# Edge scores of two attention layers: the end-of-group signal of TensorE moved from the last product to a drain

## The chip, the cores and the metric

The program runs on one core of one Trainium2 chip. The metric is the device time of one execution in microseconds, lower is better; a kernel's time is the median over its runs. Engines are named as in the profile: PE (TensorE), DVE (VectorE), ACT (ScalarE), POOL (GpSimd) and SP (SyncE).

## The reference

A graph network of four blocks over 3125 nodes with 64 features and 100,000 edges sorted by destination; each block is followed by a residual sum and a layer norm. The change lies in the last block, two GATv2 layers with five heads:

```
xl = (x @ Wl + bl).reshape(n_nodes, H, C)
xr = (x @ Wr + br).reshape(n_nodes, H, C)
e = jax.nn.leaky_relu(xl[src] + xr[dst], NEG_SLOPE)
alpha = jnp.einsum('ehc,hc->eh', e, att)
m = jax.ops.segment_max(alpha, dst, num_segments=n_nodes)
a = jnp.exp(alpha - m[dst])
...
out = jax.ops.segment_sum(a[:, :, None] * xl[src], dst, num_segments=n_nodes)
```

Every node also has an edge to itself. What is computed in the changed stage is `alpha`, the score of each edge and head (and of each self edge).

## The kernel before

The program is one long sequence of phases; each phase is a set of instruction streams, one per engine, that are ordered only by semaphores, and ends with a drain of every engine and a barrier (line 141). The changed function is `gat_edges`, called once by `gat_layer` for each of the two layers.

Edges are laid out in columns of 128 edges (one per partition). There are 816 columns, 32 of them made of nodes whose edges cross a window. A **turn** of the loop takes 24 columns; there are 34 turns a layer. Within a turn:

- **POOL** (line 2503) gathers the source rows of a column from `node_rows` in HBM into `rows_p`, with one indirect DMA per column. `rows_p` has three slots of eight columns. Before a slot is refilled POOL waits until DVE has consumed it (`used`, sent at line 2656), until SP has stored its node features to `x_src` (`stored`), and until the indices are in.
- **ACT** (lines 2594 and 2600) makes `hot_t`, a one-hot matrix of destinations within a window of 128 nodes, for half a turn (12 columns) at a time, with two buffers. Before it writes a buffer it waits until PE is done with that buffer's last group of the turn before, that is, on `made`.
- **PE** (line 2557) multiplies the one-hot matrix with the window's destination rows. These rows are split into three bf16 parts in `parts_r`, so each column takes three products of 330 output columns, accumulated in PSUM. Four columns are a **group** of 12 products; a turn has six groups, numbered 0 to 5. Groups alternate between two halves of `psZ`, so PE may start group n+1 once DVE's product of group n-1 is done (`prod`). The window of a column is known only at run time: at groups 0 and 3 PE's sequencer loads twelve numbers into registers (`pick`, line 2439), and each product's address is formed by a register operation (line 2557). In the first five turns there are two groups more, for the self edges (line 2545: three and two columns, with f32 products); they use no gathered rows.
- **DVE** adds the gathered rows to `psZ` (`add`, line 2646), reduces the group before (`reduce`, line 2669), then multiplies `psZ` after a max with the attention vector into `lz` (`product`, line 2638). The add of a group waits for `made`; the add of the first group of a slot waits for the slot's gathers too; the add of the second waits for nothing but `made` and the engine's own order.

The first five turns and the other 29 are loops of their own on the engines other than PE, which has the five written out. Where in DVE's stream a turn starts can be seen in the trace: there a reduction is followed directly by an add, with no product between them.

PE signals a group by an increment on its last product:

```
last = pe.matmul(psZ[:, n % 2, j, 0:ZH], hot[:, k, col * CE:(col + 1) * CE],
...
last.then_inc(made, 1)
```

and DVE waits with

```
v.wait_ge(made, unit(i, n, early) + EACH)
if at == 0:
    v.wait_ge(got[slot], i * (16 * KS) + 16 * KS)
```

Of the kernel before, what the change touches and what calls it, by code (L numbers as in the profile page):

```python
# [12 lines left out]
NB = N // 125  # L13
NR = P * NB
# [9 lines left out]
CE = 128  # L24
# [25 lines left out]
ZH = H * ZC  # L50
# [2349 lines left out]
def gat_edges(nc, g, h, selfs):  # L2400
# [7 lines left out]
    SB = 5  # L2408
# [8 lines left out]
    with phase(nc) as s:  # L2417
# [3 lines left out]
        locs, hot = s.sb("locs", [WR, 2, KC * CE], u8), s.sb("hot_t", [WR, 2, KC * CE], bf16)  # L2421
        lz = s.sb("lz", [P, 2, G, ZH])
        tab, hT = s.sb("tab_rows", [P, TB, ZH]), s.sb("hT", [P, NR])

        psZ = s.ps("psZ", [P, 2, G, 512])
# [5 lines left out]
        hot_made, made, added, prod, scored, neared = (s.sem(n) for n in ("hot_made", "made", "added", "prod", "scored", "neared"))  # L2431
# [6 lines left out]
        flat = lambda t: t.rearrange("k h c -> k (h c)")  # L2438
# [10 lines left out]
        with nc.Block() as block:  # L2449
# [56 lines left out]
            @block.tensor  # L2506
            def _(pe):

                def copied(by, n):
                    for e in range(2):  # L2510
                        if share(n, e):
                            pe.wait_ge(by[e], share(n, e))

                pe.sem_inc(made, EACH)
                for t, bs in enumerate(batches):
                    if t >= 4:
                        copied(hT_by, t - 3)
                    for b in bs:
                        last = pe.transpose(psZ[0:D, 1, t % 4, (b - bs.start) * P:(b - bs.start + 1) * P], h[:, b, :], g.ident[:, :])
                    last.then_inc(n_turned, 1)  # L2520
                copied(hT_by, len(batches))
                pe.wait_ge(padded, 2)
                for w in range(NWR):
                    if w >= 4:
                        copied(tab_by, w - 3)
                    pe.matmul(psZ[:, 0, w % 4, 0:ZH], hT[:, w * WR:(w + 1) * WR], flat(g.wA[:, :, :]),
                              start=True, stop=True).then_inc(n_source, 1)
                for w in range(NWR):
                    if w >= 4:
                        pe.wait_ge(n_split, w - 3)  # L2530
                    pe.matmul(psZ[:, 1, w % 4, 0:ZH], hT[:, w * WR:(w + 1) * WR], flat(g.wB[:, :, :]),
                              start=True, stop=True).then_inc(n_dest, 1)
                copied(tab_by, NWR)
                pe.wait_ge(n_split, NWR)
                pe.sem_inc(prod, 2)

                def turn(i, early):
                    for n, (kind, m) in enumerate(EARLY if early else LATE):
                        if kind:
                            lo, hi = SELF[m]  # L2540
                            if m == 0:
                                pe.wait_ge(joined, 1)
                            pe.wait_ge(prod, unit(i, n, early))
                            for b in range(lo, hi):
                                last = pe.matmul(psZ[:, n % 2, b - lo, 0:ZH], hT[:, i * SB + b:NR:NB], flat(g.wB[:, :, :]),
                                                 start=True, stop=True)
                            last.then_inc(made, 1)
                            continue
                        k, c = divmod(m, HALF)
                        if c == 0:  # L2550
                            at = pick((i * 2 + k) * KC)
                            pe.wait_ge(hot_made, i * 2 + k + 3)
                        pe.wait_ge(prod, unit(i, n, early))
                        for j in range(G):
                            col = c * G + j
                            for q in range(3):
                                last = pe.matmul(psZ[:, n % 2, j, 0:ZH], hot[:, k, col * CE:(col + 1) * CE],  # L2557
                                                 parts[:, bass.ds(at[col], 1), q, :].rearrange("p o c -> p (o c)"),
                                                 start=q == 0, stop=q == 2)
                        last.then_inc(made, 1)  # L2560

                for i in range(ST):
                    turn(i, True)
                with pe.Fori(ST, NK // 2) as i:
                    turn(i, False)
# [671 lines left out]
```

## Time and profile before

| | us |
|---|---|
| median of 3 runs | 7766.42 |
| lowest and highest run | 7758.99, 7787.47 |
| span of the profiled execution | 7865.6 |

The profiled execution is one more execution, recorded by the hardware profiler; of it the span is given, and no other time. Busy times of engines are sums over the span: PE 4297.8 us (55%), DVE 4772.7 (61%), ACT 2362.7 (30%), POOL 3733.3 (47%).
```text
span 7865.6 us, 104440 instructions
## 1 busy us (share of the span) xinstructions
PE 4297.8 (55%) x26852; PEld 3458.2 (44%) x26923; DVE 4772.7 (61%) x7334; ACT 2362.7 (30%) x3661; POOL 3733.3 (47%) x4217
## 2 busy tenths in 40 slices
PE   5777777310279545555535444444695444444397
PEld 2677776310179545555523222222683222222396
DVE  4666666688521156566547666666665766666675
ACT  5444444117322145555522111111222111111121
POOL 3666566100200166666625555553654555655363
PEclk9555555555589777777767666666896766666696
DMA  8677777895578533233225656564654666656462
GB/s 313 191 219 212 222 203 226 228 236 191 215 250 307 183 112 115 96 117 114 91 72 147 159 152 156 154 157 119 135 134 114 157 158 155 160 150 158 100 140 75
DMA packets 1472089, 1296.30 MB, mean 165 GB/s; under 512 B 1257993, under 2 KB 1297567, under 8 KB 1459038
## 3 DMA queue, kind: packets, MB, share of 16 engines
q1 hardware_dynamic: 902378, 671.59, 28.5%
q0 software_dynamic: 167008, 441.69, 21.0%
q10 hardware_dynamic: 402580, 181.62, 8.4%
q8 instruction: 48, 0.79, 0.0%
q14 instruction: 75, 0.61, 0.0%
HBM read 942.23 MB, written 351.27 MB: 164 GB/s over the span
## 5 line engine op out<-in xcount | busy, mean ns | idle before, releaser
L2503 POOL DMA_INDIRECT rows_p<-node_rows,stage_i x1632 | 1546.5, 948 | 1228.0 <-issue 978.9
L2557 PE MATMUL psZ<-parts_r,hot_t 128*128 x4896 | 1164.3, 402 | 1360.5 <-DVE lz L2638 867.7
L2557 PEld LDWEIGHTS psZ<-parts_r,hot_t 128*128 128x128 bf16 x4896 | 590.0, 121 | 1938.6 <-issue 1624.4
L2646 DVE TENSOR_TENSOR psZ<-psZ,rows_p 128x1320 f32<-128x1320 f32 x408 | 626.5, 1536 | 768.9 <-remote 283.0
L731 POOL DMA_INDIRECT rows_s<-hpx,hpST x784 | 741.4, 946 | 486.4 <-issue 203.8
L1961 POOL DMA_INDIRECT both<-table,srcI x784 | 741.9, 946 | 431.5 <-issue 211.1
L749 PE MATMUL psP<-window,pair_hot 128*128 x3136 | 701.9, 416 | 249.0 <-ACT pair_hot L771 146.6
L749 PEld LDWEIGHTS psP<-window,pair_hot 128*128 128x128 f32 x3136 | 672.8, 325 | 279.2 <-issue 279.0
L828 DVE SCALAR_TENSOR_TENSOR pair_run<-pair_run,same_c,psP 128x64 f32<-128x64 f32 x1568 | 440.2, 281 | 469.1 <-PE psP L749 209.1
L2953 PE MATMUL ps_steps<-A,xs 128*65 128x125 f32 x5184 | 578.8, 272 | 137.8 <-DVE A L2971 93.1
L2638 DVE SCALAR_TENSOR_TENSOR lz<-psZ,att 128x1320 f32<-128x1320 f32 (+2 forms) x428 | 642.6, 1501 | 8.4
L2953 PEld LDWEIGHTS ps_steps<-A,xs 128*65 128x65 f32 x5184 | 562.9, 138 | 153.5 <-issue 151.5
L2600 ACT ACTIVATE hot_t<-near 128x1536 bf16<-128x1536 bf16 x136 | 201.9, 1485 | 1418.1 <-DMA first_tab<-homeX_i 417.4
L2669 DVE TENSOR_REDUCE sj<-lz 128x1320 f32 x408 | 621.1, 1522 | 11.0
L1997 PE MATMUL psZ<-w,bothT 128*128 128x128 f32 x1568 | 374.3, 328 | 214.0 <-ACT bothT L2030 158.2
L2971 DVE TENSOR_TENSOR A<-hotw,aw 128x3000 f32<-128x3000 f32 x108 | 354.6, 3283 | 195.4 <-PE ps_steps L2953 183.9
L2927 POOL TENSOR_TENSOR acc<-acc,part_w 65x125 f32 x648 | 316.5, 488 | 248.1 <-ACT part_w L2886 155.3
L1724 PE MATMUL psY<-parts,tile 128*125 128x192 bf16 x4200 | 388.5, 251 | 72.9 <-DVE parts L1764 45.2
L2594 ACT ACTIVATE near<-locs,node_lane 128x1536 bf16<-128x1536 uint8 x136 | 214.5, 1577 | 705.6 <-DMA locs<-loc_rows 429.7
L1724 PEld LDWEIGHTS psY<-parts,tile 128*125 128x125 bf16 x4200 | 364.3, 140 | 75.4 <-issue 42.9
L1999 PE MATMUL psZ<-w,eaT 128*128 128x128 f32 x1568 | 370.9, 325 | 8.6 <-issue 8.6
L630 ACT ACTIVATE tile<-psA 128x500 bf16<-128x500 f32 (+1 forms) x294 | 161.6, 562 | 644.5 <-remote 421.8
(545 smaller groups left out, 7260.0 us busy)
## 6 DMA issues: line engine op xcount, KB each, us to landing
tile<-adj SPq DMA_DIRECT2D x168, 781.2 KB, 4.9
xs<-x_src SPq DMA_DIRECT2D x432, 128.0 KB
x_src<-rows_p SPq DMA_DIRECT2D x204, 256.0 KB
hpx<-stage ACTq DMA_DIRECT2D x25, 2048.0 KB
window<-hpx SPq DMA_DIRECT2D x196, 256.0 KB
dst_runs<-pair_run SPq DMA_DIRECT2D x28, 1792.0 KB
eaT<-in_ea SPq DMA_DIRECT2D x28, 1792.0 KB
adj<-tile SPq DMA_DIRECT2D x42, 781.2 KB
```

Source lines behind the costliest of these rows:

```text
L731: pool.indirect_dma_start(rows[:, k, j, :], None, g.hpx, bass.IndirectOffsetOnAxis(g.hpST[:, x * K + j:x * K + j + 1], 0)).then_inc(got[k] ...
L749: last = pe.matmul(pair_sum(n, j), hot[:, n % 2, j * CE:(j + 1) * CE], window[:, n % 2, bass.ds(rel[j], 1), :].rearrange("p o c -> p (o c) ...
L828: v.scalar_tensor_tensor(run[:, k, at, :], run[:, k, at - 1, :] if at else run[:, 1 - k, PC - 1, :], same[:, k, at:at + 1], pair_sum(n, j) ...
L1724: last = pe.matmul(psY[0:TC, k % B, 0:3 * D], tile[:, k, b, :], parts[:, b].rearrange("p n c -> p (n c)"), start=b == 0, stop=b == NB - 1)
L1961: pool.indirect_dma_start(both[:, x % 2, j, D:2 * D], None, g.table, bass.IndirectOffsetOnAxis(g.srcI[:, x * K + j:x * K + j + 1], 0)).the ...
L1997: pe.matmul(psZ[:, q % 4, j, :], bothT[:, q % 2, j, :], w1[:, :], start=False, stop=False, skip_group_check=True)
L2503: pool.indirect_dma_start(rows[:, k, j, :], None, g.node_rows, bass.IndirectOffsetOnAxis(stage[:, k, j:j + 1], 0)).then_inc(got[k], 16)
L2557: last = pe.matmul(psZ[:, n % 2, j, 0:ZH], hot[:, k, col * CE:(col + 1) * CE], parts[:, bass.ds(at[col], 1), q, :].rearrange("p o c -> p ( ...
L2638: return v.scalar_tensor_tensor(out, src, 0.0, att.unsqueeze(1).to_broadcast([P, n, ZH]), ALU.max, ALU.mult)
L2646: v.tensor_tensor(here, here, rows[:, slot, at * G:(at + 1) * G, 0:ZH], ALU.add).then_inc(added, 1)
L2669: v.tensor_reduce(out, lz[:, n % 2, 0:size, :].rearrange("p g (h c) -> p g h c", c=ZC), X, ALU.add).then_inc(scored, 1)
L2953: last = pe.matmul(slot(k, j), xs[:, k, j, e, 0:D + 1], A[:, k, j * EG + e, :], start=e == 0, stop=e == EG - 1)
```

## The change

The increment of `made` is taken off the last product of each group, edge groups and self groups alike, and put on a drain instruction behind it. A drain is executed by PE's sequencer and completes when PE has finished what was issued before it. Nothing else is changed; line numbers stay as they were.

```diff
--- before.py
+++ after.py
@@ -2542,9 +2542,9 @@
                                 pe.wait_ge(joined, 1)
                             pe.wait_ge(prod, unit(i, n, early))
                             for b in range(lo, hi):
-                                last = pe.matmul(psZ[:, n % 2, b - lo, 0:ZH], hT[:, i * SB + b:NR:NB], flat(g.wB[:, :, :]),
+                                pe.matmul(psZ[:, n % 2, b - lo, 0:ZH], hT[:, i * SB + b:NR:NB], flat(g.wB[:, :, :]),
                                                  start=True, stop=True)
-                            last.then_inc(made, 1)
+                            pe.drain().then_inc(made, 1)
                             continue
                         k, c = divmod(m, HALF)
                         if c == 0:
@@ -2554,10 +2554,10 @@
                         for j in range(G):
                             col = c * G + j
                             for q in range(3):
-                                last = pe.matmul(psZ[:, n % 2, j, 0:ZH], hot[:, k, col * CE:(col + 1) * CE],
+                                pe.matmul(psZ[:, n % 2, j, 0:ZH], hot[:, k, col * CE:(col + 1) * CE],
                                                  parts[:, bass.ds(at[col], 1), q, :].rearrange("p o c -> p (o c)"),
                                                  start=q == 0, stop=q == 2)
-                        last.then_inc(made, 1)
+                        pe.drain().then_inc(made, 1)
 
                 for i in range(ST):
                     turn(i, True)
```

## Rows read from the trace of the kernel before

**Rows 1.** The page: span, and two groups of part 5 (columns named below)

Columns: line, engine, operation, out<-in, count; busy us, mean ns of one; idle us before, releaser.

```profile
span 7865.6 us, 104440 instructions
...
L2503 POOL DMA_INDIRECT rows_p<-node_rows,stage_i x1632 | 1546.5, 948 | 1228.0 <-issue 978.9
L2557 PE MATMUL psZ<-parts_r,hot_t 128*128 x4896 | 1164.3, 402 | 1360.5 <-DVE lz L2638 867.7
```

**Rows 2.** L2503 in each layer: duration min/median/max in ns, first and last start

```profile
L2503 POOL DMA_INDIRECT rows_p<-node_rows,stage_i x816: 942/948/958, 4106.3 to 5424.6; - x164
...
L2503 POOL DMA_INDIRECT rows_p<-node_rows,stage_i x816: 942/948/978, 5980.9 to 7301.8; - x164
```

**Rows 3.** L2646 over the span, and what ended the idle time before it (us, times)

```profile
L2646 DVE TENSOR_TENSOR psZ<-psZ,rows_p x408: 1529/1534/1542, 4152.5 to 7323.1; 128x1320 f32<-128x1320 f32 x136
...
  remote: 283.0, 58
  DMA first_tab<-homeX_i: 281.9, 52
  issue: 133.0, 22
  PE psZ L2557: 71.0, 17
```

**Rows 4.** Timeline of all engines, 4600 to 4660 us: start, us, engine, line, idle before

```profile
4608.52 1.53 DVE L2646 TENSOR_TENSOR psZ<-psZ,rows_p 128x1320 f32<-128x1320 f32 x1
...
4610.17 1.53 DVE L2638 SCALAR_TENSOR_TENSOR lz<-psZ,att 128x1320 f32<-128x1320 f32 x1
...
4611.62 1.53 DVE L2646 TENSOR_TENSOR psZ<-psZ,rows_p 128x1320 f32<-128x1320 f32 x1
...
4611.85 2.57 PE L2557 MATMUL psZ<-parts_r,hot_t 128*128 x12 [2.92 <-issue]
...
4614.50 1.52 DVE L2638 SCALAR_TENSOR_TENSOR lz<-psZ,att 128x1320 f32<-128x1320 f32 x1
4614.92 0.95 POOL L2503 DMA_INDIRECT rows_p<-node_rows,stage_i  x1 [0.30 <-issue]
...
4616.16 3.48 PE L2557 MATMUL psZ<-parts_r,hot_t 128*128 x12 [1.75 <-issue]
4616.17 0.95 POOL L2503 DMA_INDIRECT rows_p<-node_rows,stage_i  x1 [0.30 <-issue]
...
4619.29 1.48 ACT L2600 ACTIVATE hot_t<-near 128x1536 bf16<-128x1536 bf16 x1 [11.29 <-remote]
4619.30 1.54 DVE L2646 TENSOR_TENSOR psZ<-psZ,rows_p 128x1320 f32<-128x1320 f32 x1 [3.27 <-remote]
...
4627.99 1.54 DVE L2646 TENSOR_TENSOR psZ<-psZ,rows_p 128x1320 f32<-128x1320 f32 x1 [4.29 <-remote]
...
4630.37 0.95 POOL L2503 DMA_INDIRECT rows_p<-node_rows,stage_i  x1 [5.73 <-issue]
...
4641.17 1.86 PE L2557 MATMUL psZ<-parts_r,hot_t 128*128 x12 [2.45 <-DVE lz L2638]
...
4654.95 1.54 DVE L2646 TENSOR_TENSOR psZ<-psZ,rows_p 128x1320 f32<-128x1320 f32 x1 [9.16 <-remote]
...
4657.37 0.94 POOL L2503 DMA_INDIRECT rows_p<-node_rows,stage_i  x1 [5.53 <-DVEq L2656]
```

**Rows 5.** L2656, DVE's release of a slot: who waited for it (us, times)

```profile
  POOL rows_p L2503: 249.1, 38
```

**Rows 6.** PE's sequencer by line, whole span; the last row from 4616 to 4628 us

```profile
L141 PEldq DRAIN  x47: 8/8/131, 23.4 to 7865.1; - x47
...
L2439 PEldq TENSOR_LOAD <-firsts x136: 3/848/1368, 4146.8 to 7307.2; - x136
...
L2564 PEldq COMPARE_BRANCH  x58: 16/208/838, 4359.5 to 7320.5; - x58
...
L2557 PEldq FUSED_REGOPS  x4896: 2/46/1422, 4149.1 to 7320.3; - x196
...
L2557 PEldq FUSED_REGOPS  x21: 3/46/724, 4616.1 to 4627.9; - x21
```

**Rows 7.** Busy time, granted clock (PEclk) and DMA share in the two gather stretches

```profile
4106.00:5425.00 1319.00, 610.55 (x2491) 313.81 (x2490) 906.86 (x660) 224.92 (x179) 772.66 (x816) 0.68 0.60 155
5981.00:7302.00 1321.00, 617.17 (x2488) 308.94 (x2488) 904.88 (x658) 224.25 (x177) 772.46 (x816) 0.68 0.60 154
```

## What the change should do

> **What bounds the kernel now.** I read the page first. The kernel is no chain of one engine: over the span of 7865.6 us no engine is busy for more than 61%, and the changed line L2557 (PE, 1164.3 us busy in 4896 products) has 1360.5 us of idle time before its products [rows 1]. So PE is not short of time there, and only the moment at which its signal `made` arrives can matter. The costliest group of the page is the gather of L2503 on POOL, in the same loop.
>
> Next I read that gather by layer. Each layer issues 816 gathers, from 4106.3 to 5424.6 us and from 5980.9 to 7301.8 us, so 1318.3 and 1320.9 us [rows 2]. In the timeline two gathers that wait for nothing start 1.25 us apart (4614.92 and 4616.17) [rows 4]. 816 x 1.25 is 1020 us, so the layers spend 298 and 301 us in which POOL had no leave to issue, 599 us in both. DVE's own work is less: one group of four columns costs it an add, a reduction and a product, 4.33 us from one product to the next (4610.17 to 4614.50), so 26.0 us a turn of six groups against 30.1 us for POOL's 24 gathers [rows 4].
>
> What takes POOL's leave away? L2646, the add that reads what PE made, has 768.9 us of idle time before it in 149 stalls: 283.0 + 281.9 + 133.0 + 71.0 us, and the profile names mostly releasers that are not in the loop (remote, a DMA of another stage) [rows 3]. The timeline tells more [rows 4]. The turn starts with the add at 4608.52; 4611.62 is the add of its group 1, 4619.30 of group 2, 4627.99 of group 3. Group 2 was multiplied from 4611.85 for 2.57 us, so its products end at 4614.42 by the profile; its add starts at 4619.30. ACT's hot_t, which waits for `made` of that same group and for no gather, starts at 4619.29, 0.01 us away. Group 3 is the second group of its slot, so its add waits for `made` alone: its products end at 4616.16 + 3.48 = 4619.64, its add starts at 4627.99, 8.35 us later. After it POOL starts the next refill at 4630.37, having been idle for 5.73 us. The same again with the group of 4641.17: end 4643.03, add 4654.95, POOL 4657.37. So **PE's signal arrives 5 to 12 us after the products end** in these places, and through DVE's release of the slot (POOL waited for it by name for 249.1 us [rows 5]) it holds back the gathers. The layer is bound by POOL plus these late signals.
>
> **The change part by part.** Removed: the increment on the last product of 428 groups (2 layers of 204 edge groups and 10 self groups). Added: 428 drains on PE, each with the increment. No order changes, on no engine; no product, load or transfer is added.
>
> *The drain itself.* PE's drains at the ends of phases take 8 ns in the median and 131 ns at most [rows 6]. 428 x 0.008 is 3 us, 428 x 0.131 is 56 us, as bounds; I take 10 us of issue, nearly all in PE's idle time.
>
> *What queues behind it.* Now PE's sequencer issues register operations and loads while the last products still run. After a drain it can't: the wait for `prod`, and at groups 0 and 3 the table load of `pick` (848 ns median, 136 of them) and at the back edge the branch (208 ns, 58 of them), start only when PE is empty [rows 6]. Cover: PE gets leave for the next group every 4.33 us, and a group takes 1.86 us at the full clock and 3.48 us at the low one [rows 4]; the mean grant is 0.68 in these stretches, so 0.36 of the time at 2.4 GHz and 0.64 at 1.2 GHz [rows 7]. Low clock with a table load: 0.14 (from product to PE's start) + 3.48 + 0.1 (drain) + 0.85 + about 0.2 of register work is 4.8 us, 0.4 to 0.5 us over the cover. Without a load: 3.7 us, covered. So at most 136 x 0.45 x 0.64 = 39 us, and 58 x 0.3 x 0.64 = 11 us for back edges, 50 us if all lay on the path; at the low end none does, since DVE has 4.1 us a turn to spare against POOL. I take 10 us.
>
> *When the signal arrives.* This is the open term. Before, PE's array sent it; now its sequencer does, after the array is empty. No drain occurs inside a gather loop of this trace, so I bound it: if the new signal is never late, all 599 us of POOL's lost leave could go; if it is as late as before, 0; if lateness also delays the next group, it costs (below). What speaks for one common cause is that PE's sequencer is itself slowed in the same stretch: from 4616 to 4628 us one of its register operations took 724 ns against a median of 46 [rows 6]. A drain with a signal would pass by the same sequencer. I take 0 for this term as the likeliest.
>
> The Trainium skill (PSUM — Partial Sum Buffer, Engine vs sequencer instructions) says that an increment on the matmul fires at its completion, and that a drain waits until the engine is fully idle; by that rule the drained signal can never come before the old one, and the forecast would be no gain in any case. The trace does not contradict the second half, but shows the old signal 8.35 us behind the profile's end of the products [rows 4]. The skill (Perfetto Trace Analysis, Tensor Engine Instruction) also calls that end an estimate, so the products themselves might be late; then the drain waits for them as well.
>
> Sum: 10 + 10 + 0 = +20 us. The sum is made on the profiled execution; its span is 99 us (1.3%) above the median of 7766.42 us, and I carry the difference over unscaled: **7786 us**. That the median is so near also says that most of the lost time is no product of profiling: without it two layers alone would be 599 us shorter.
>
> **The rivals.** About 0.5% (39 us) is what a measurement can tell from no change.
>
> *A. Same lateness, hidden drain (the forecast).* 7769 to 7872 us by the bounds above (3 + 0 to 56 + 50). Chance 0.42, of it 0.36 within 0.5% and 0.06 slower.
>
> *B. The sequencer's signal is not held up.* Then DVE's stalls go and POOL issues nearly without a break. For it: only PE's signals are late here; DVE's product ending at 4616.02 released PE at 4616.16 in the same stretch [rows 4]. Against it: the slowed register operations. The most is 599 us (7167 us); the store of x_src and the waits for slots remain, so I take 0.7 of it, 419 us: about 7350 us, and from 7200 to 7700 us. Chance 0.33.
>
> *C. Lateness in series (the other side).* Before, PE multiplied group 3 from 4616.16 while the signal of group 2 was still out until 4619.3. If the drain must wait for whatever is held up, group 3 starts only at 4619.3, 3.1 us later, and its own late signal counts from there. It decides where two stalls follow each other, as groups 2 and 3 do; in the printed stretch that is one case in a turn, and with 68 turns, some without, I take 45: 45 x 3.1 is 140 us. If it struck two times a turn it were 420 us. So 7786 + 140 = 7926 us, range 7830 to 8200. Chance 0.20.
>
> *D. The edit does nothing,* since the signal was late for a reason of the receiver (DVE and ACT read the semaphore late) and the drain is hidden: 7766 us. Against it, both started within 0.01 us of each other. Chance 0.05.
>
> **How the numbers follow.** Faster is B, 0.33. Within 0.5% is 0.36 of A and 0.05 of D, 0.41 in all. Slower is 0.06 of A and 0.20 of C, 0.26. The likeliest case gives 7786 us; its own range is 7760 to 7850, the measurement's own spread below and most of the bounds above. Cases of both signs hold half of the chance, so the range must reach into B and C: from 7300 us (a third of B is below, 0.11) to 7950 us (somewhat under half of C is above, 0.08).
>
> **What would show it.** In the changed profile: 428 drains of PE at L2547 and L2560 (if no such rows, D's first half). A: the idle time before L2646 stays near 769 us and the two gather stretches near 1320 us; table loads of L2439 start after the last product's end instead of beside it. B: the idle time before L2646 falls under 200 us and the gather stretches to 1050 to 1150 us; then the forecast was wrong on what holds the signal. C: PE's groups start with the late adds, not 3 us ahead of them, the stalls before L2646 grow to 900 us or more, and the gather stretches are longer than 1380 us. The stages outside the two stretches should not move at all; if they did, the comparison would be one of something else.

## The result and the profile after

The change makes the kernel slower by about one and a half per cent.

| | before | after |
|---|---|---|
| median, us | 7770.84 | 7897.47 |
| runs | 4, 7758.99 to 7787.47 | 4, 7876.42 to 7906.69 |
| ratio after / before | | 1.0149, 95% interval 1.0129 to 1.0169 |
| span of the profiled execution, us | 7865.6 | 7896.1 |

The medians are 127 us apart, the two spans only 30. (The quotient of the two medians is 1.0163; it lies inside the interval of the ratio.) The profiled execution of before is none of its four runs and lies 95 us above their median, that of after within 2 us of its own. So the two profiles understate the difference, and they are read for how things go, less for how much. The ratios further down leave out four executions of 7285 to 12792 us, which took far longer than the others of the same kernel.

The page of the changed kernel, span and groups of part 5 (columns as in [rows 1]):

```profile
span 7896.1 us, 104938 instructions
...
L2503 POOL DMA_INDIRECT rows_p<-node_rows,stage_i x1632 | 1542.2, 945 | 1294.7 <-issue 1049.2
L2557 PE MATMUL psZ<-parts_r,hot_t 128*128 x4896 | 1089.6, 391 | 1482.0 <-issue 1069.9
...
L2646 DVE TENSOR_TENSOR psZ<-psZ,rows_p 128x1320 f32<-128x1320 f32 x408 | 626.4, 1535 | 819.1 <-PEq L2560 689.8
```

No instruction of the two groups became longer: a product takes 391 ns in the mean (before 402), a gather 945 (before 948) [rows 1]. What grew is idle time: before the add of L2646 from 768.9 us [rows 3] to 819.1. Its releasers are now named, and all but 22 stalls end by the drain (us, times):

```profile
  PEq L2560: 689.8, 144
  issue: 128.9, 22
```

The gathers of the two layers, first and last start, against [rows 2]:

```profile
L2503 POOL DMA_INDIRECT rows_p<-node_rows,stage_i x816: 940/946/955, 4085.5 to 5431.7; - x164
...
L2503 POOL DMA_INDIRECT rows_p<-node_rows,stage_i x816: 940/946/971, 5981.6 to 7334.0; - x164
```

1346.2 and 1352.4 us instead of 1318.3 and 1320.9, 59 us more in both. The stages outside did not grow: together they are 29 us shorter, which fits a profiled execution of before that was long everywhere, and not an effect of the change. The drain itself is the surprising row (min/median/max in ns; below it, who waited for it):

```profile
L2560 PEldq DRAIN  x408: 219/2052/14652, 4128.5 to 7352.2; - x136
...
  ACT hot_t L2600: 1529.6, 130
  DVE psZ L2646: 689.8, 144
```

A drain that takes 8 ns in the median at the ends of phases [rows 6] takes 2052 ns in the median here and up to 14652. One of them alone, in the stretch from 4610 to 4620 us:

```profile
L2560 PEldq DRAIN  x1: 9148/9148/9148, 4613.0 to 4613.0; - x1
```

and what stands around it in the timeline (columns as in [rows 4]):

```profile
4607.02 1.53 DVE L2646 TENSOR_TENSOR psZ<-psZ,rows_p 128x1320 f32<-128x1320 f32 x1
...
4611.34 1.53 DVE L2646 TENSOR_TENSOR psZ<-psZ,rows_p 128x1320 f32<-128x1320 f32 x1
...
4611.56 1.86 PE L2557 MATMUL psZ<-parts_r,hot_t 128*128 x12 [2.13 <-DVE lz L2638]
...
4614.21 1.52 DVE L2638 SCALAR_TENSOR_TENSOR lz<-psZ,att 128x1320 f32<-128x1320 f32 x1
...
4622.16 1.54 DVE L2646 TENSOR_TENSOR psZ<-psZ,rows_p 128x1320 f32<-128x1320 f32 x1 [6.43 <-issue]
...
4622.47 3.48 PE L2557 MATMUL psZ<-parts_r,hot_t 128*128 x12 [9.05 <-issue]
...
4627.91 1.48 ACT L2600 ACTIVATE hot_t<-near 128x1536 bf16<-128x1536 bf16 x1 [18.63 <-PEq L2560]
4627.91 1.54 DVE L2646 TENSOR_TENSOR psZ<-psZ,rows_p 128x1320 f32<-128x1320 f32 x1 [1.34 <-PEq L2560]
...
4629.67 3.48 PE L2557 MATMUL psZ<-parts_r,hot_t 128*128 x12 [3.72 <-ACT hot_t L2600]
4630.29 0.94 POOL L2503 DMA_INDIRECT rows_p<-node_rows,stage_i  x1 [5.15 <-issue]
...
4637.65 1.86 PE L2557 MATMUL psZ<-parts_r,hot_t 128*128 x12 [2.05 <-issue]
...
4652.92 1.54 DVE L2646 TENSOR_TENSOR psZ<-psZ,rows_p 128x1320 f32<-128x1320 f32 x1 [11.12 <-PEq L2560]
...
4654.30 3.48 PE L2557 MATMUL psZ<-parts_r,hot_t 128*128 x12 [14.79 <-issue]
...
4657.83 1.54 DVE L2646 TENSOR_TENSOR psZ<-psZ,rows_p 128x1320 f32<-128x1320 f32 x1 [0.51 <-PEq L2560]
```

The adds of 4607.02 and 4611.34 are those of groups 2 and 3; the products from 4611.56 are group 4. By the profile they end at 4613.42. The drain behind them starts at 4613.0, takes 9148 ns, and so ends at 4622.15; DVE's add starts at 4622.16, 8.74 us after the products' modelled end, as late as the signals of the kernel before [rows 4]. So it is not the way of the signal that is slow: PE's own sequencer does not see PE as finished until then.

The second thing to see is the next line of PE. Group 5 had leave from 4615.73 on (the product of 4614.21 + 1.52), but starts at 4622.47. In the kernel before it would have started at once, as the group of 4616.16 did [rows 4]. Its signal then comes at 4627.91, 1.96 us after its end at 4625.95, and DVE has stood still once more. And at 4629.67 PE starts group 0 of the next turn, 1.76 us after the drain: in between lie the branch (208 ns from 4628.1) and the table load (848 ns from 4628.5), with register work around them. The profile names ACT's `hot_t` as the releaser there, but group 0 reads the other buffer, which was ready since 4607.67. At 4652.92 a signal arrives 13.4 us after the products of 4637.65 ended; the next group starts 1.38 us later, ends at 4657.78, and its add waits for it (0.51 us).

### The profile page after: what moved, and what is told of

Same layout as the page of the kernel before. It is cut to its first block and busy times, and to the rows that moved or that the text cites. A ratio compares the mean times of both kernels' runs of the same rounds, so it can differ in the third digit from the quotient of the medians.

```text
span 7896.1 us, 104938 instructions
## 1 busy us (share of the span) xinstructions
PE 4257.9 (54%) x26922; PEld 3469.0 (44%) x26923; DVE 4772.0 (60%) x7334; ACT 2359.9 (30%) x3661; POOL 3724.4 (47%) x4217
## 5 line engine op out<-in xcount | busy, mean ns | idle before, releaser
L2503 POOL DMA_INDIRECT rows_p<-node_rows,stage_i x1632 | 1542.2, 945 | 1294.7 <-issue 1049.2
L2557 PE MATMUL psZ<-parts_r,hot_t 128*128 x4896 | 1089.6, 391 | 1482.0 <-issue 1069.9
L2557 PEld LDWEIGHTS psZ<-parts_r,hot_t 128*128 128x128 bf16 x4896 | 583.8, 119 | 1993.2 <-issue 1675.2
L2646 DVE TENSOR_TENSOR psZ<-psZ,rows_p 128x1320 f32<-128x1320 f32 x408 | 626.4, 1535 | 819.1 <-PEq L2560 689.8
L731 POOL DMA_INDIRECT rows_s<-hpx,hpST x784 | 739.5, 943 | 476.2 <-issue 205.9
```

The lines of the kernel that those rows point to most:

```text
L731: pool.indirect_dma_start(rows[:, k, j, :], None, g.hpx, bass.IndirectOffsetOnAxis(g.hpST[:, x * K + j:x * K + j + 1], 0)).then_inc(got[k] ...
L2503: pool.indirect_dma_start(rows[:, k, j, :], None, g.node_rows, bass.IndirectOffsetOnAxis(stage[:, k, j:j + 1], 0)).then_inc(got[k], 16)
L2646: v.tensor_tensor(here, here, rows[:, slot, at * G:(at + 1) * G, 0:ZH], ALU.add).then_inc(added, 1)
```

## The experiments

Three theories were put to the test. **S (series):** a drain holds PE until its own late completion, so the next group no longer runs under the wait. **L (late signal):** the drain's signal reaches the others later than a product's would. **T (table loads):** the sequencer's work behind a drain is exposed. All are short edits of `gat_edges`.

The runs fell on different chips, and that turned out to matter more than the change: the same kernel before took 7771, 7885 and 7775 us in three sets of runs and 6823 and 6816 us in two others. Every ratio below is against the kernel before on the same chip in the same set. I call the first kind of chip "late" and the second "prompt", after what PE's completions do on them. No chip is known to have served in two sets, so the words name what a set showed and not a proven property of the chip.

**e1: a drain behind each group that signals nothing.**

```diff
                         last.then_inc(made, 1)
+                        pe.drain()
```

(the same behind the self groups)

> The kernel before with a drain behind every group that signals nothing; the last product signals as before. Theory S (series): the cost comes from PE being held at the drain until its own late completion, so the next group is multiplied only after it; then this costs the same as the change, 7870 to 7910 us, and PE's groups start late as in the changed kernel. Theory L (late signal): the drain's own signal reaches DVE and ACT later than a product's would; then the time is that of before, 7760 to 7790 us.

Measured on a prompt chip: 6824.70 us against 6823.01, ratio 1.0010 (1.0001 to 1.0020). It can't tell S from L there. But its profile, of an execution as fast as the kernel before, shows what is different on such a chip. The add's idle time (us, times) in its profile:

```profile
L2648 DVE TENSOR_TENSOR psZ<-psZ,rows_p x408: 1525/1530/1542, 3687.7 to 6274.7; 128x1320 f32<-128x1320 f32 x136
...
  DMA rows_p<-node_rows,stage_i: 186.6, 102
  PE psZ L2558: 20.2, 15
```

Not 769 us but 207, and the releaser is the gather of the rows itself. PE's completions come on time, POOL is the bound, and 428 drains cost at most 0.2%.

**e2 and e3: drains with the signal at groups 2 and 5 only (136), and at all others only (292).** The edit of e2 is shown; e3 has the two choices the other way round, and the drain behind the self groups.

```diff
-                        last.then_inc(made, 1)
+                        (pe.drain() if m % HALF == HALF - 1 else last).then_inc(made, 1)
```

> Drain with signal only at groups 2 and 5 of each turn (136 of 428), behind which the table load, and at 5 the loop's branch, come; the other groups signal by their last product. Theory T (table loads): the cost is the sequencer's work that no longer runs beside the products; then nearly all of the change's +127 us is here, 7870 to 7900 us. Theory S: the cost goes by the number of drains that are passed late, a third of them, so 7800 to 7830 us.

> The complement: drain with signal at groups 0, 1, 3, 4 and the self groups (292 of 428), product signal at 2 and 5. Theory T: near the kernel before, 7770 to 7790 us. Theory S: two thirds of the change's cost, 7840 to 7870 us.

Same prompt chip: ratios 1.0005 (0.9996 to 1.0014) and 1.0002 (0.9993 to 1.0011). Both misses: neither theory's price shows where PE is not late. What follows is only that T by itself, without late completions, costs nothing that can be measured (at most 0.14%) in a loop bound by POOL.

**e4: the kernel before with one gather per slot.**

```diff
-                        for j in range(KS):
+                        for j in range(1):
```

(with the waits on the gathers lowered to match, and `rows_p` set to zero once)

> The kernel before with one gather per slot instead of eight (the other rows are zero, so the edge scores leave out the source part of 7 columns in 8). If it is POOL's stream of gathers that holds PE's completions back, the late signals go: the idle time before L2646 falls from 769 us to under 100 us, and the two stretches become DVE-bound, 34 x 26 us and some, about 950 us each instead of 1320, so about 7050 us in all. If lateness has another cause (the SP stores, the products themselves), the stalls stay above 400 us and the time above 7300 us.

6620.67 us, ratio 0.9705 (0.9688 to 0.9723), on the same prompt chip: DVE-bound as expected (the 7050 us were meant for a late chip), but no test of the cause, since nothing was late in the kernel before either.

**e5 and e6: the changed kernel, and the silent drain, side by side again.**

> The changed kernel itself once more. In the runs just made the kernel before took 6823 us where it had taken 7771, and its gathers followed each other without long pauses: PE's signals were not late. If the cost of the drains hangs on late signals (theory S), the change costs 1.5% only where the kernel before takes about 7770 us, and under 0.2% where it takes about 6820 us. If the cost is the drains' own work (theory T), it is 100 us or more in either case.

> The silent drain again, beside the changed kernel. Where the kernel before takes about 7770 us: theory S says the same as the changed kernel, theory L the same as before. Where it takes about 6820 us: all three the same, which tells nothing between S and L.

This was a late chip, with 7884.69 us for the kernel before. The changed kernel took 7966.92 us, ratio 1.0106 (1.0080 to 1.0132), the silent drain 7975.36 us, ratio 1.0116 (1.0090 to 1.0143). That decides between S and L: a drain that carries no signal costs the same as one that does, within the two intervals. In the profile of e6, the drain, and the add that now again waits for the last product:

```profile
L2562 PEldq DRAIN  x408: 343/2079/14845, 4129.1 to 7405.1; - x136
...
L2648 DVE TENSOR_TENSOR psZ<-psZ,rows_p x408: 1526/1531/1542, 4131.0 to 7407.8; 128x1320 f32<-128x1320 f32 x136
...
  DMA first_tab<-homeX_i: 374.7, 52
  remote: 370.0, 45
  PE psZ L2558: 65.2, 58
  issue: 59.1, 14
```

869 us of idle time before the add: the product's own signal is as late as ever, and the drain beside it takes up to 14845 ns. Here both can be seen on the same group. In all 146 stalls of more than 0.5 us before the add, the add starts between 1.4 us before and 0.1 us after the end of that group's silent drain, in 104 of them within 0.1 us. So the signal of the product and the end of the drain are late together.

**e7 and e8: e2 and e3 again.**

> The 136 drains at groups 2 and 5 (table load or branch behind them) again. Only a set of runs in which the kernel before takes 7750 us or more tells anything, since at 6820 us no drain costs. There the change cost 82 to 127 us. Theory T (the loads no longer run beside the products): 70 to 120 us. Theory S (a drain holds PE until its late completion, a cost per drain passed late): a third, 25 to 45 us.

> The other 292 drains again. Where the kernel before takes 7750 us or more: theory T 0 to 20 us, theory S two thirds of the change's cost, 55 to 85 us.

A prompt chip (6815.73 us for the kernel before): ratios 0.9990 (0.9977 to 1.0002) and 1.0000 (0.9989 to 1.0011). Nothing new.

**e9: e4 again.**

> The kernel before with one gather per slot instead of eight (source part of 7 columns in 8 left out, rows zero). At 6820 us for the kernel before it took 6621 us, DVE-bound. If POOL's stream of gathers is what makes PE's completions late, then also where the kernel before takes 7750 us or more the stalls before the add are short (under 100 us in all) and this takes about 7885 less 2 x 375 us less, about 7050 us, since only the late signals of the other stages stay. If they have another cause, it stays above 7300 us.

6614.32 us (two runs), ratio 0.9700 (0.9681 to 0.9719), prompt chip. It serves as the reference for e11. The adds of its two layers, first and last start:

```profile
L2648 DVE TENSOR_TENSOR psZ<-psZ,rows_p x204: 1526/1531/1542, 3686.8 to 4600.4; 128x1320 f32<-128x1320 f32 x102
...
L2648 DVE TENSOR_TENSOR psZ<-psZ,rows_p x204: 1527/1531/1542, 5158.9 to 6071.9; 128x1320 f32<-128x1320 f32 x102
```

**e10: POOL waits for the landing of each slot's gathers.**

```diff
                                                     bass.IndirectOffsetOnAxis(stage[:, k, j:j + 1], 0)).then_inc(got[k], 16)
+                        pool.wait_ge(got[k], i * (16 * KS) + 16 * KS)
```

> The kernel before with one wait more: POOL, after the eight gathers of a slot, waits until they have landed before it goes on. At 6820 us for the kernel before this costs 34 x 3 x 2 x 2.5 us, about 500 us. Where the kernel before takes 7750 us or more: if lateness builds up over gathers that follow each other for more than 10 us and clears in a pause, the pauses are then short ones and PE is on time, and each layer takes 102 x (10 + 2.5), 1275 us instead of 1320 to 1350: 50 to 150 us faster. If lateness does not need a long stream, the waits add up: 300 us slower or more.

7399.48 us, ratio 1.0856 (1.0838 to 1.0874): 584 us, near the 500 expected for a prompt chip; POOL's idle time that ended with its own gathers' landing was 413.7 us in 136 waits by name. Whether it would pay on a late chip stays untried. Against the 584 us that it costs here, the expectation hoped for 50 to 150 us there.

**e11: the changed kernel with one gather per slot.**

> The changed kernel (428 drains) with one gather per slot instead of eight (source part of 7 columns in 8 left out, rows zero). DVE then bounds the loop and PE's cover is thinnest. With product signals this took 6621 and 6614 us beside a kernel before of about 6820 us. If the table loads behind a drain are exposed as I worked out (136 x 0.45 x 0.64 + 11 us), 6660 to 6675 us; if the drains are covered, 6610 to 6630 us. On a chip where the kernel before takes 7750 us or more: if POOL's gathers are what makes PE late, about 7050 to 7100 us and short stalls before the add; if not, above 7300 us.

A late chip (7775.31 us for the kernel before): 7029.67 us, ratio 0.9042 (0.9027 to 0.9057). That is 20 us under the range expected if POOL's gathers are the cause, and far from the 7300 us and more expected if they are not. First and last add of the two layers:

```profile
L2648 DVE TENSOR_TENSOR psZ<-psZ,rows_p x204: 1526/1530/1542, 4096.1 to 5010.1; 128x1320 f32<-128x1320 f32 x102
...
L2648 DVE TENSOR_TENSOR psZ<-psZ,rows_p x204: 1525/1530/1542, 5571.0 to 6484.0; 128x1320 f32<-128x1320 f32 x102
```

Their stretches are 914.0 and 913.0 us against 913.6 and 913.0 in e9, which has product signals and a prompt chip. So with one gather in eight PE is on time even on a late chip: none of the 428 drains ends more than 0.02 us after the modelled end of its products. And 428 drains, with every load and branch behind them, cost under 1 us in a loop that DVE bounds, as far as one profile of each kernel tells. The add's waits for a drain are (us, times):

```profile
  PEq L2562: 16.8, 13
```

**e12: the 136 drains at groups 2 and 5, third try.**

> The 136 drains at groups 2 and 5 once more, for a chip where the kernel before takes 7750 us or more: theory T 70 to 120 us slower, theory S 25 to 45 us slower. Where it takes about 6820 us: no difference, as twice before.

On the same late chip as e11: 7855.97 us against 7775.31, ratio 1.0107 (1.0090 to 1.0124), +81 us. The lowest of this interval, 0.90%, is more than half of the highest for the full change, 1.69%. By the count of drains S expected 25 to 45 us, and that version of S falls. The number is T's, but T as exposed work alone falls by e11 and the prompt chips. The other 292 drains never ran on a late chip, nor did the full change on this one, so what the rest would have added is open. The rows of e12:

```profile
L2560 PEldq DRAIN  x136: 223/2058/14332, 4121.1 to 7305.2; - x136
...
L2646 DVE TENSOR_TENSOR psZ<-psZ,rows_p x408: 1526/1531/1542, 4116.3 to 7307.9; 128x1320 f32<-128x1320 f32 x136
...
  PEq L2560: 410.1, 54
  remote: 145.0, 31
  DMA first_tab<-homeX_i: 135.8, 33
  PE psZ L2557: 73.0, 49
```

The traces give a measure of what both theories are about: the time for which PE was held, worked out for each group as the start of its first product, less the end of the DVE product that frees its half of PSUM, less the usual 0.14 us, and counted where it is over 0.15 us:

| | held, us | groups | until the drain ended | behind it |
|---|---|---|---|---|
| before | 11 | 13 | | |
| changed kernel | 967 | 245 | 844 | 123 |
| e5, the changed kernel again | 1005 | 236 | | |
| e6, silent drain | 1072 | 247 | 948 | 124 |
| e11, one gather in eight | 47 | 67 | 14 | 33 |
| e12, groups directly behind a drain | 522 | 70 | 417 | 105 |
| e12, other groups | 38 | 50 | | |

The changed kernel and the silent drain hold PE alike, and seven eighths of the time is the wait for the drain to end; the branch, load and register work behind it are the rest. In e11, with the same 428 drains but PE on time, 47 us are left. In e12, with a third of the drains, the sum is 560 us, 0.58 of the changed kernel's. The full change cost 82 and 127 us on its two chips; 0.58 of that is 48 to 74 us, against 81 (70 to 96) measured on another chip. So held time comes nearer than the count of drains, but it is no exact price: most of the 967 us never reached the end of the layer.

Why a third of the drains makes more than half of the held time is not shown. It is no property of groups 2 and 5 themselves: taken as the end of the drain less the modelled end of its products, the lateness is 1006 us over all drains of the changed kernel, and 297 of it at these two groups, under a third. In e12 the same two groups show 667 us. How much of the 81 us is the load and how much the late completion, these runs don't separate either; of the held time the load's side is 105 of 522 us.

## Why the prediction was right and where it was wrong

The time fell inside the range, but the forecast did not foresee what happened: it was 7786 us, measured were 7897, outside the 7760 to 7850 us of its likeliest case, and slower had a chance of 0.26 in all. The range from 7300 to 7950 us held it because it had to reach into rivals on both sides; that is width, and not insight. By its own steps:

- *The bound.* Right. POOL's gathers plus late signals bound the two layers; on the prompt chips, where no signal is late, the gathers run from 3657.9 to 4684.2 us in e7, 1026.3 us for 816, against 1318.3 us. The kernel before is 950 us faster there, in part in other stages: the gathers of L731 take 991 us in e7 (196.9 to 1188.2) and 1224 in the profile before (196.3 to 1420.7). The 1020 us taken from the 1.25 us step was near.
- *"It is no product of profiling".* Right in the main: runs without profile differ by the same 950 us between chips. What the 95 us of the profiled before over its own median are, no run shows. The kernel before took 7885 us in another set without any profile, so another chip would explain them as well as profiling.
- *The drain itself, 3 to 56 us.* The row it rested on, drains at the ends of phases (8 ns), was the wrong neighbour: an idle PE is drained there. Inside the loop the drain lasts as long as PE's completion is late. Where PE is on time, all 428 add under 1 us to the path (e11), less than the 10 us taken.
- *What queues behind it, 0 to 50 us, taken 10.* Without late completions 0 (e11, prompt chips), even bound by DVE; the cover of 4.33 us held. With them it is part of the loss: 1.76 us from drain to first product at the back edge and 1.38 us at group 3, 123 of the 967 us for which PE was held.
- *When the signal arrives: "I take 0 for this term".* This is the step that failed. Its first half was right: the drain's signal is as late as the product's, and rival B is dead. Its second half, that an equal lateness costs nothing, was not: the same lateness now holds PE too, for 844 us up to the drains' ends, and the time grew by 127 us. The bound "if lateness also delays the next group, it costs" was named and priced as rival C, and given 0.20.
- *Rival C.* Right as mechanism (e6 against e5). In size it came near by luck: 140 us taken, 127, 82 and, for the silent drain, 91 us measured. Its sum was 45 cases of 3.1 us, each paid in full; held were 245 groups for 3.9 us in the mean, most of it covered by other waits. Its own marks were too strong: the stalls before the add went to 819 us, not 900, and the gathers to 1346 and 1352 us, not over 1380. They were set from a profile of before that was itself long, which may be part of it.
- *The argument from the slowed register operations.* It pointed the wrong way. In the changed kernel, where the sequencer stands at the drain instead, they are nearly gone: of the 4896 register operations of L2557, 263 took over 300 ns before and 13 after (the longest 1422 and 1395 ns). The branch at the back edge, up to 838 ns before, now takes 223 at most, and the table load, as low as 3 ns before, 845 at least [rows 6]:

```profile
L2439 PEldq TENSOR_LOAD <-firsts x136: 845/850/1557, 4124.7 to 7341.4; - x136
...
L2564 PEldq COMPARE_BRANCH  x58: 76/208/223, 4350.0 to 7354.4; - x58
```

That fits a sequencer that was slowed by PE's backlog, and no obstacle that a sequencer's signal alone would meet; it was read from these rows and not tested. The Trainium skill's rule (PSUM — Partial Sum Buffer, Engine vs sequencer instructions), that a drain waits until the engine is fully idle, was the better guide: the drain of 9148 ns agrees with it, and that wait is the cost.

## What to carry to other kernels

A signal on the last product lets PE's sequencer and its next group go on while the completion is still out; a drain, with or without a signal, ends that run-ahead. Where completions were prompt, and each group had 4.33 us of another engine's work as cover, the drains here were free; where they were late, a drain put the wait in series with the next group, and 428 of them cost 82 to 127 us. And before a wait is priced from a trace, the kernel should be timed on a second chip: the stall that is edited may exist on one and not on the other.

## What the runs showed of the hardware

PE's completions can be seen up to 14 us after the modelled end of the products (13.4 us for the group of 4637.65), on some chips and not on others, with the same program: 7771, 7885 and 7775 us against 6823 and 6816. On the one late chip where it was tried, it needs POOL's stream of indirect gathers: with one in eight left, the completions of this loop were on time (e11). That run took away the issuing on POOL and the transfers together, and does not tell which of the two matters. It left the other stages as they were: the stage of L731 still took 1208 us for its 784 gathers (196.5 to 1404.9 us), against 1002 us (193.3 to 1195.5) in e1. What in the chip or its surroundings makes the difference, no run here shows.
